# A Mamba and SwiGLU layer on one core: squares of the norms spread over beats, softplus split over two beats, one exponential moved up to the table load

## The chip, the cores and the metric

The kernel runs on one core of one Trainium2 chip. The metric is the device time of one execution in microseconds. An engine is called by its name in the profile: PE (TensorE matmul), PEld (its weight load), DVE (VectorE), ACT (ScalarE), POOL (GpSimd), SP (SyncE).

## What is computed

The input has 8192 tokens (4 sequences of 2048) of 256 channels. One layer of two halves is applied to it.

```python
# half 1: selective state space block (D_INNER = 512, N_STATE = 16, DT_RANK = 16, K_CONV = 4)
x_in, res = split(x @ W_in)
x_conv = silu(causal_dw_conv(x_in, conv_w, conv_b))             # u
dt, Bm, Cm = split(x_conv @ W_x)
delta = softplus(dt @ W_dt + b_dt)
h = exp(delta * A) * h + delta * Bm * x_conv                    # scan over tokens, 16 states a channel
y = sum_n(h * C) + u * D
x1 = layernorm(x + (y * silu(res)) @ W_out)
# half 2: gated feed-forward block (HIDDEN = 768, integer weights / 127)
out = layernorm(x1 + (silu(x1 @ Wg.T) * (x1 @ Wu.T)) @ Wd.T)
```

Softplus is computed as max(v, 0) + ln(1 + exp(-|v|)): Relu, Abs, Exp and Ln on ACT. A norm takes the mean (`minus_mean`), four Squares with an accumulator output (one for each 128 tokens), then rstd = exp(-0.5 ln(var + eps)), then a scale and a shift on POOL.

## The kernel before

The tokens are cut into 16 chunks of 512. A step of the loop handles one chunk, and a step has 64 beats: 16 states times 4 blocks of 128 channels. At each beat ACT computes da = exp(A * delta) for one state and block (`exp`, L1052), POOL computes dbu (L1185), and DVE runs the recurrence over 512 tokens (`scan`, L1360, tile `h`). After four beats PE turns the four blocks of the state around (tiles `ht_upper`, `ht_lower`, L699); ACT weighs the upper half with C (`weigh`, L1061, tile `gt`), DVE sums the lower half (L1372, tile `acc`), PE turns the weighed upper half back onto `y_upper` (L724).

All other matmuls are called fills. They go through two PSUM banks in turn (`fill_banks`) at beats written out by hand in `FILL_AT`, and are read at the beats of `READ_AT`. In step i they serve the projections, the convolution and softplus of chunk i+1 (the front) and the output projection, the norms and the feed-forward block of chunk i-1 (the back). A fill waits until its bank's holder before it has been read.

Every engine runs its instructions in the order in which the program lists them. On ACT a beat lists: the exponential of that beat, then `sums` (the weighing, at every beat with beat % 4 = 1 or 3), the norms, the reads of the back, the reads of the front, and at the beats 35 and 45 (`SILUS`) the silu work. There ACT first computes the exponentials of the next two beats (`AHEAD = 2`) into SBUF (`da_ahead`), loads the table of silu (L1129), runs one silu instruction, and in the beat behind it the second, and loads the table of exp and ln again (L1140). The beat that follows (38 or 48) begins with its own exponential. da has two banks, so exp of beat b waits for the scan of beat b-2; dbu has four buffers.

The second norm of a chunk (`which` = 1) falls into the second step behind it, beats 64 and above of `BEAT` counted from the step before: 65 is beat 1, 86 is beat 22. Of the first norm PE transposes the result in the fill `x1t0` at beat 28.

In the traces below a scan is numbered by its beat: the step that is read runs from 929.25 us (scan of beat 0) to 1041.47 us. Of its scans, that of beat 24 begins at 968.93, of 26 at 971.95, of 30 at 978.19, of 38 at 994.23 and of 48 at 1012.75.

Of the kernel before, what the change touches and what calls it, by code (L numbers as in the profile page):

```python
# [12 lines left out]
ACT = mybir.ActivationFunctionType  # L13
# [3 lines left out]
TT = T // P  # L17
# [38 lines left out]

BEAT = {"times u": [53, 55, 58, 63], "x1 low": [33, 34], "mean": [22, 65], "rstd": [23, 65], "shift": [26, 86],
        "norm": [29, 86], "silu uz": 35, "silu gate": 45, "y upper": [6, 6], "times z": [11, 12, 12, 15]}

FIRST_FILLS = ["xin0", "xin1", "xin2", "xin3", "conv2", "conv0", "conv1", "conv3", "dtb", "dt0", "dt1", "ct", "dt2", "dt3"]  # L60

# [13 lines left out]
AHEAD = 2  # L75
SILUS = sorted(BEAT[name] for name in ("silu uz", "silu gate"))
# [2 lines left out]

assert not [n for n, at in READ_AT.items() if n[:2] == "dt" and n != "dtb" and at - 1 in SILUS]  # L80
assert not [b for b in BEAT["rstd"] if b - 1 in SILUS or b - 65 in SILUS]


def due(names, beat):

    return [name for name in names if READ_AT[name] == beat]
# [10 lines left out]
def in_steps(at, beat, first, last):  # L97

    return not (first if beat < at else last)


def tiles_due(kind, beat):

    return [n for n, at in enumerate(BEAT[kind]) if at == beat]


def mamba_swiglu(nc, x, x_t, w_in, conv_w, conv_b, w_x, w_dt, b_dt, a_log, d_skip, w_out, w_gate_t, w_up_t,
# [9 lines left out]
    KK, DB, HB = DM // P, DI // P, HID // P  # L117
# [21 lines left out]
    with ExitStack() as ctx:  # L139
# [32 lines left out]
        u = sb("u", [P, 2, DB, T])  # L172
        z = sb("z", [P, 2, DB, T])
        delta = sb("delta", [P, 2, DB, T])
# [18 lines left out]
        xr = sb("xr", [P, 2, TT, DM])  # L193
# [96 lines left out]
        def ahead(beat):  # L290

            for start in SILUS:
                if start < beat <= start + AHEAD:
                    return beat - start - 1
            return None
# [588 lines left out]
        def _(act):  # L884
# [3 lines left out]
            def front(c, par, beat):  # L888
                if beat == 0:


                    start = T + (HALO if c % PER_SEQ == 0 else 0)
                    after(act, xin_ready, c * (DB + 1))
                    copy(xin[:, :, 0:HALO], xin[:, :, start:start + HALO]).then_inc(xin_ready, 1)
                read_front(c, par, due(F_FILLS, beat))

            def read_front(c, par, names):
                for name in names:
                    m = int(name[-1]) if name[-1].isdigit() else 0
                    b = front_bank(c, name)  # L900
                    act.wait_ge(fp_ready, front_filled(c, name))
                    if name[:3] == "xin":
                        act.wait_ge(xin_ready, c * (DB + 1) + 1)
                        copy(xin[:, m, HALO:HALO + T], b[:, :]).then_inc(xin_ready, 1)
                    elif name[:3] == "res":
                        if isinstance(c, int) and c == 1 and m == 0:

                            act.wait_ge(w_ready, 6)
                        after(act, lower_done, (c - 2) * DP + m // 2 + 1)
                        copy(z[:, par, m, :], b[:, :]).then_inc(res_raw, 1)  # L910
                    elif name[:4] == "conv":

                        after(act, lower_done, (c - 2) * DP + m // 2 + 1)
                        nc.scalar.activation(u[:, par, m, :], b[:, :], ACT.Identity,
                                             bias=convb_s[:, m:m + 1]).then_inc(conv_raw, 1)
                    elif name == "dtb":
                        after(act, b_written, 16 * c)
                        nc.scalar.activation(xd[:, :], b[0:XD, :], ACT.Identity, bias=ones_row[:, 0:1])\
                            .then_inc(xd_ready, 2)
                    elif name == "ct":  # L920
                        copy(ct[:, par, :, :], b[:, 0:TT * NS].rearrange("p (t n) -> p t n", n=NS))\
                            .then_inc(ct_ready, 1)
                    else:

                        d = delta[:, par, m, :]
                        done = (c * DB + m) * 3

                        if c:
                            nc.scalar.activation(du[:, par, m, :], b[:, :], ACT.Relu).then_inc(relu_ready, 1)
                        nc.scalar.activation(d, b[:, :], ACT.Abs).then_inc(softplus_step, 1)  # L930
                        act.wait_ge(softplus_step, done + 1)
                        nc.scalar.activation(d, d, ACT.Exp, scale=-1.0).then_inc(softplus_step, 1)
                        act.wait_ge(softplus_step, done + 2)
                        nc.scalar.activation(d, d, ACT.Ln, bias=1.0).then_inc(softplus_step, 1)


            def silu_u(c, par):
# [12 lines left out]
            def minus_mean(c, which):  # L950
                act.wait_ge((res1_done, res2_done)[which], (c + which + 1) * TT)
                if which:
                    act.wait_ge(nmr_ready, 2 * c + 1)
                elif isinstance(c, int):
                    after(act, nmr_ready, 2 * c)
                nc.scalar.activation(neg_mean[:, :], row_sum[:, which, :], ACT.Copy, scale=-1.0 / DM)\
                    .then_inc(mean_ready, 1)

            def reciprocal_std(c, par, which):

                if which:
                    act.wait_ge(x1_ready, TT * (c + 1))
                elif isinstance(c, int):
                    after(act, o_ready, TT * c)
                act.wait_ge(mean_ready, 2 * c + which + 1)
                for t in range(TT):
                    nc.scalar.activation(squares[:, t, :], xr[:, par, t, :], ACT.Square, bias=neg_mean[:, t:t + 1],
                                         accum_out=sq[:, t:t + 1]).then_inc(sq_done, 1)
                act.wait_ge(sq_done, TT * (2 * c + which + 1))
                nc.scalar.activation(rstd[:, :], sq[:, :], ACT.Ln, bias=eps_s[:, 0:1], scale=1.0 / DM)\  # L970
                    .then_inc(rstd_step, 1)
                act.wait_ge(rstd_step, 2 * (2 * c + which) + 1)
                nc.scalar.activation(rstd[:, :], rstd[:, :], ACT.Exp, scale=-0.5).then_inc(rstd_step, 1)
# [58 lines left out]
            def norms(c, par, beat):  # L1032
                for which in tiles_due("mean", beat):
                    minus_mean(c, which)
                for which in tiles_due("rstd", beat):
                    reciprocal_std(c, par, which)

            def exp(i, par, beat):
                n, m = beat // DB, beat % DB
# [68 lines left out]
            def step(i, par):  # L1108
                first, last = [isinstance(i, int) and i == c for c in (0, NCH - 1)]
                for beat in range(NH):  # L1110

                    if ahead(beat) is None and not (first and beat < 2):
                        exp(i, par, beat)
                    sums(i, par, beat, first, False)
                    if not (isinstance(i, int) and i < 2):
# [22 lines left out]
                        silu_z(0, 0)  # L1138
                    if beat - 1 in SILUS:
                        nc.scalar.preload_act_table_set(EXP_SET)  # L1140

            steps(step)
            for beat in range(NH):
# [382 lines left out]
```

## Time and profile before

| | |
|---|---|
| median of 3 runs | 1870.64 us (1870.13 to 1873.51) |
| profiled execution, span | 1865.8 us |
| a step of 64 beats in that execution (steps 1 to 14) | 112.2 to 112.8 us |
| busy: PE, DVE, POOL, ACT | 1715.3, 1705.4, 1651.8, 1636.9 us |
| scan L1360 on DVE | x1024, 1269 ns each |
| exp da L1052 on ACT | x1024, 689 ns each |
| weigh gt L1061 on ACT | x512, 681 ns each |
| Square L967 on ACT | x120, 498 ns, and 190 ns for each read of the accumulator |
| table loads L1129, L1140 | x32 each, 1283 ns |

The span is the profiled execution from its first to its last instruction; the median of the runs is 4.8 us above it. An idle time in brackets behind an instruction is that of its engine just before it, with what ended it. Ends of PE's instructions are modelled, so that its rows show overlaps: four 128-column transposes are given 0.60 us but start every 0.44 us.

### The profile page before, as it was taken

The numbers are of one execution on the slowest core, as the hardware profiler recorded it, in microseconds if no ns is written. First come the engines' busy times: TensorE is split into PE (matmuls) and PEld (weight loads), VectorE is DVE, ScalarE is ACT, GpSimd is POOL, SyncE is SP. The second block draws the span as 40 slices with busy tenths as digits, with TensorE's granted clock in tenths as the row PEclk, the third lists the DMA queues.
The fourth block names the chain that finished last, engine by engine and source line by source line (L and its number), as shares of the span: only waits on it lengthen the run. The fifth ranks groups of instructions, "written<-read, shape, count | busy, mean of one in ns | idle before, by whom it ended". The sixth has DMA issues, their size and how long they took to land.

```text
span 1865.8 us, 32487 instructions
## 1 busy us (share of the span) xinstructions
PE 1715.3 (92%) x10128; PEld 1287.3 (69%) x10128; DVE 1705.4 (91%) x1958; ACT 1636.9 (88%) x2769; POOL 1651.8 (89%) x1629
## 2 busy tenths in 40 slices
PE   8879898998989999898998989999898998988788
PEld 3546676776767677676776767677676776767667
DVE  5989999999999999999999999999999999999994
ACT  5798988989899898998989899898998989898774
POOL 3989899998989989899898999989899898989970
PEclk9999999999999999999999999999999999999999
DMA  7213123141231314214141231313214041221100
GB/s 240 109 46 136 47 71 134 35 159 47 103 102 58 125 47 142 63 60 145 35 151 55 99 106 58 125 47 135 70 58 147 36 147 57 87 96 41 62 23 24
DMA packets 82107, 164.56 MB, mean 88 GB/s; under 512 B 10369, under 2 KB 28033, under 8 KB 81938
## 3 DMA queue, kind: packets, MB, share of 16 engines
q1 hardware_dynamic: 80498, 160.90, 25.1%
q8 instruction: 85, 1.39, 0.3%
q10 hardware_dynamic: 1440, 1.58, 0.3%
q14 instruction: 84, 0.69, 0.1%
HBM read 87.47 MB, written 8.91 MB: 52 GB/s over the span
## 4 chain that ended last, share of the span: by engine, by line
PE 65%; ACT 22%; POOL 7%; issue 4%; DVE 2%; DMA 0%; DVEq 0%; SPq 0%; ACTq 0%; POOLq 0%
PE fill L524 10%; PE ht_upper L699 9%; PE ht_lower L699 9%; PE y_upper L724 8%; PE fill L639 8%; POOL dbu L1185 6%; PE fill L608 5%; PE fill L629 5%; ACT da L1052 4%; ACT gt L1061 3%; PE fill L539 3%; ACT L1140 2%; ACT L1129 2%; PE fill L578 2%; ACT kb L948 2%
## 5 line engine op out<-in xcount | busy, mean ns | idle before, releaser
L1185 POOL TENSOR_TENSOR dbu<-du,brep 128x512 f32<-128x512 f32 x1024 | 1310.6, 1306 | 152.3 <-DVE h L1360 128.7
L1360 DVE TENSOR_TENSOR_SCAN h<-da,carry,dbu 128x512 f32<-128x512 f32 x960 | 1186.9, 1269 | 92.5 <-ACT da L1052 90.7
L1052 ACT ACTIVATE da<-delta,a_s 128x512 f32<-128x512 f32 x960 | 655.7, 689 | 97.2 <-DVE h L1360 89.8
L1061 ACT ACTIVATE gt<-ht_upper,ct 128x512 f32<-128x512 f32 x512 | 348.5, 681 | 62.7 <-PE ht_upper L699 55.7
L699 PE MATMUL ht_upper<-ident,h 128*128 128x128 f32 x2048 | 317.7, 278 | 67.7 <-DVE h L1360 57.3
L699 PEld LDWEIGHTS ht_upper<-ident,h 128*128 128x128 f32 x2048 | 245.9, 143 | 185.9 <-DVE h L1360 102.8
L1372 DVE SCALAR_TENSOR_TENSOR acc<-ht_lower,ct,acc 128x512 f32<-128x512 f32 x480 | 348.6, 726 | 22.4 <-PE ht_lower L699 22.4
L699 PE MATMUL ht_lower<-ident,h 128*128 128x128 f32 x2048 | 317.0, 278 | 39.4 <-DVE acc L1372 34.9
L724 PE MATMUL y_upper<-ident,gt 128*128 128x128 f32 x2048 | 316.6, 278 | 0.0
L699 PEld LDWEIGHTS ht_lower<-ident,h 128*128 128x128 f32 x2048 | 243.8, 143 | 103.0 <-issue 50.4
L724 PEld LDWEIGHTS y_upper<-ident,gt 128*128 128x128 f32 x2048 | 245.8, 143 | 72.1 <-ACT gt L1061 39.6
L524 PE MATMUL fill<-xt_s,win_s 128*128 128x512 f32 x456 | 217.5, 594 | 0.1
L639 PE MATMUL fill<-wd_s,kb 128*128 128x256 f32 x720 | 180.4, 380 | 0.7 <-DVE xr L1272 0.5
L639 PEld LDWEIGHTS fill<-wd_s,kb 128*128 128x128 f32 x720 | 125.8, 190 | 19.2 <-DVE xr L1272 8.0
L629 PE MATMUL fill<-x1t,wg_s 128*128 128x512 f32 x360 | 128.8, 471 | 3.3 <-ACT kb L1000 3.2
L608 PE MATMUL fill<-wout_s,kb 128*128 128x256 f32 x480 | 118.5, 380 | 0.0
L629 PE MATMUL fill<-x1t,wu_s 128*128 128x512 f32 x360 | 110.2, 428 | 4.1 <-ACT delta L930 4.1
L524 PEld LDWEIGHTS fill<-xt_s,win_s 128*128 128x128 f32 x456 | 76.8, 190 | 51.5 <-issue 50.8
L1360 DVE TENSOR_TENSOR_SCAN h<-da_ahead,carry,dbu 128x512 f32<-128x512 f32 x64 | 101.0, 1617 | 0.0
L608 PEld LDWEIGHTS fill<-wout_s,kb 128*128 128x128 f32 x480 | 87.6, 190 | 10.4 <-issue 0.4
L307 POOL TENSOR_TENSOR du<-delta,u 128x512 f32<-128x512 f32 x60 | 76.5, 1276 | 4.7
L629 PEld LDWEIGHTS fill<-x1t,wg_s 128*128 128x128 f32 x360 | 69.2, 222 | 16.5 <-ACT kb L1000 9.3
(189 smaller groups left out, 1871.9 us busy)
## 6 DMA issues: line engine op xcount, KB each, us to landing
brep<-b_rows SPq DMA_DIRECT2D x127, 512.0 KB, 3.8
xs<-xin SPq DMA_DIRECT2D x242, 256.0 KB, 2.5
xr<-x SPq DMA_DIRECT2D x16, 512.0 KB, 4.2
xt_s<-x_t SPq DMA_DIRECT2D x15, 512.0 KB, 5.1
out<-xr SPq DMA_DIRECT2D x15, 512.0 KB, 3.9
win_s<-w_in SPq DMA_DIRECT2D x2, 512.0 KB, 5.0
h<-xin SPq DMA_DIRECT2D x4, 256.0 KB, 4.0
h<-xin ACTq DMA_DIRECT2D x4, 256.0 KB, 4.5
```

What stands on the lines that cost most here:

```text
L307: unit.tensor_tensor(du[:, par, m, :], d, u[:, par, m, :], ALU.mult).then_inc(du_ready, 1)
L524: mm = nc.tensor.matmul(front_bank(c, name)[:, :], win_s[:, k, m * P:(m + 1) * P], xt_place(c)[:, k, :], start=(k == 0), stop=(k == KK - 1))
L608: mm = nc.tensor.matmul(fill_bank(name)[:, 0:DM], kb[:, m, t * P:(t + 1) * P], wout_s[:, m, :], start=(m == 0), stop=(m == DB - 1))
L629: mm = nc.tensor.matmul(fill_bank(name)[:, :], w[:, k, n * P:(n + 1) * P], x1t[:, half, k, :], start=(k == 0 and half == 0), stop=(k == KK ...
L639: mm = nc.tensor.matmul(fill_bank(name)[:, 0:DM], kb[:, n, t * P:(t + 1) * P], wd_s[:, n, :], start=(n == 0), stop=(n == HB - 1))
L699: mm = nc.tensor.transpose(bank[:, m * P:(m + 1) * P], h[:, n % 2, m, t * P:(t + 1) * P], ident[:, :])
L724: mm = nc.tensor.matmul(y_upper[m // 2][:, (m % 2) * HALF + k * P:(m % 2) * HALF + (k + 1) * P], lhsT=gt[:, (n * UPPER + k) % GT, m * P:(m ...
L1052: nc.scalar.activation(dst[:, :], delta[:, par, m, :], ACT.Exp, scale=a_s[:, m, n:n + 1])\
L1061: nc.scalar.activation(gt[:, (n * UPPER + k) % GT, :], ht_upper[:, :], ACT.Copy, scale=ct[:, par, k, n:n + 1])\
L1185: nc.gpsimd.tensor_tensor(dbu[:, beat % DBU, :], du[:, par, m, :], brep[:, n // PIECE % 2, n % PIECE, :], ALU.mult).then_inc(dbu_ready, 1)
L1360: nc.vector.tensor_tensor_scan(h[:, n % 2, m, 0:T], da[beat % 2][:, :] if slot is None else da_ahead[:, slot, :], dbu[:, beat % DBU, :], c ...
L1372: nc.vector.scalar_tensor_tensor(out=acc[:, par, k, :], in0=ht_lower[:, :], scalar=ct[:, par, UPPER + k, n:n + 1], in1=acc[:, par, k, :], ...
```

## The change

Three things are done, all in the order of ACT's instructions, with POOL's `shift` following the first.

1. The four Squares of a norm no longer stand in one beat with the Ln and Exp of rstd. First norm: mean 22, squares 22, 23, 24, 25, rstd 25 (was 23), shift 27 (was 26), norm 29 as before. Second norm: mean 76 (was 65), squares 77, 79, 81, 82, rstd 83 (was 65), shift 84 (was 86), norm 86 as before.
2. Exp and Ln of softplus of a `dt` block move from the beat that reads it (49, 51, 55, 59) to the next beat, behind that beat's exponential da. For chunk 0 they stay.
3. The exponential of beats 38 and 48, the first that is not computed ahead of a silu, moves from the start of its beat to the end of beat 36 or 46, directly behind the table load.

The number and sizes of all instructions stay the same.

```diff
-BEAT = {"times u": [53, 55, 58, 63], "x1 low": [33, 34], "mean": [22, 65], "rstd": [23, 65], "shift": [26, 86],
-        "norm": [29, 86], "silu uz": 35, "silu gate": 45, "y upper": [6, 6], "times z": [11, 12, 12, 15]}
+BEAT = {"times u": [53, 55, 58, 63], "x1 low": [33, 34], "mean": [22, 76], "square": [(22, 23, 24, 25), (77, 79, 81, 82)],
+        "rstd": [25, 83], "shift": [27, 84], "norm": [29, 86], "silu uz": 35, "silu gate": 45, "y upper": [6, 6],
+        "times z": [11, 12, 12, 15]}
...
+AFTER_SILU = [start + AHEAD + 1 for start in SILUS]
...
+def squares_due(which, beat):
+
+    return [t for t, at in enumerate(BEAT["square"][which]) if at == beat]
...
                 read_front(c, par, due(F_FILLS, beat))
+                for m in range(DB):
+                    if READ_AT[f"dt{m}"] + 1 == beat:
+                        softplus(c, par, m)
...
                         if c:
                             nc.scalar.activation(du[:, par, m, :], b[:, :], ACT.Relu).then_inc(relu_ready, 1)
-                        nc.scalar.activation(d, b[:, :], ACT.Abs).then_inc(softplus_step, 1)
-                        act.wait_ge(softplus_step, done + 1)
-                        nc.scalar.activation(d, d, ACT.Exp, scale=-1.0).then_inc(softplus_step, 1)
-                        act.wait_ge(softplus_step, done + 2)
-                        nc.scalar.activation(d, d, ACT.Ln, bias=1.0).then_inc(softplus_step, 1)
+                        nc.scalar.activation(delta[:, par, m, :], b[:, :], ACT.Abs).then_inc(softplus_step, 1)
+                        if not c:
+                            softplus(c, par, m)
+
+            def softplus(c, par, m):
+
+                d = delta[:, par, m, :]
+                done = (c * DB + m) * 3
+                act.wait_ge(softplus_step, done + 1)
+                nc.scalar.activation(d, d, ACT.Exp, scale=-1.0).then_inc(softplus_step, 1)
+                act.wait_ge(softplus_step, done + 2)
+                nc.scalar.activation(d, d, ACT.Ln, bias=1.0).then_inc(softplus_step, 1)
...
+            def square(c, par, which, t):
+
+                act.wait_ge(mean_ready, 2 * c + which + 1)
+                nc.scalar.activation(squares[:, t, :], xr[:, par, t, :], ACT.Square, bias=neg_mean[:, t:t + 1],
+                                     accum_out=sq[:, t:t + 1]).then_inc(sq_done, 1)
+
+            def reciprocal_std(c, which):
 
                 if which:
                     act.wait_ge(x1_ready, TT * (c + 1))
                 elif isinstance(c, int):
                     after(act, o_ready, TT * c)
-                act.wait_ge(mean_ready, 2 * c + which + 1)
-                for t in range(TT):
-                    nc.scalar.activation(squares[:, t, :], xr[:, par, t, :], ACT.Square, bias=neg_mean[:, t:t + 1],
-                                         accum_out=sq[:, t:t + 1]).then_inc(sq_done, 1)
...
                 for which in tiles_due("mean", beat):
                     minus_mean(c, which)
+                for which in range(2):
+                    for t in squares_due(which, beat):
+                        square(c, par, which, t)
                 for which in tiles_due("rstd", beat):
-                    reciprocal_std(c, par, which)
+                    reciprocal_std(c, which)
...
-                    if ahead(beat) is None and not (first and beat < 2):
+                    if ahead(beat) is None and beat not in AFTER_SILU and not (first and beat < 2):
                         exp(i, par, beat)
...
                     if beat - 1 in SILUS:
                         nc.scalar.preload_act_table_set(EXP_SET)
+                        exp(i, par, beat + AHEAD)
```

## Rows read from the trace of the kernel before

**Rows 1.** Page, parts 1 and 4: busy time of each engine; shares of the chain.
```profile
PE 1715.3 (92%) x10128; PEld 1287.3 (69%) x10128; DVE 1705.4 (91%) x1958; ACT 1636.9 (88%) x2769; POOL 1651.8 (89%) x1629
...
PE 65%; ACT 22%; POOL 7%; issue 4%; DVE 2%; DMA 0%; DVEq 0%; SPq 0%; ACTq 0%; POOLq 0%
```

**Rows 2.** Busy in three stretches of one step: span, PE, PEld, DVE, ACT, POOL, clock, DMA.
```profile
929.20:980.60 51.40, 50.61 (x311) 36.22 (x308) 48.40 (x55) 44.78 (x89) 50.81 (x55) 1.00 0.42 143
980.60:1015.10 34.50, 28.59 (x163) 21.61 (x163) 31.05 (x32) 34.21 (x48) 26.96 (x25) 0.95 0.15 50
1015.10:1041.40 26.30, 26.22 (x158) 21.84 (x159) 25.61 (x34) 23.09 (x39) 25.99 (x25) 1.00 0.13 42
```

**Rows 3.** Timeline of PE, beats 31 to 36: start, duration, work, idle time before it.
```profile
980.60 0.66 PE L617 MATMUL fill<-ident,xr 128*128 128x128 f32 x4 [0.73 <-ACT z L886]
...
984.57 0.63 PE L699 MATMUL ht_lower<-ident,h 128*128 128x128 f32 x4 [1.38 <-DVE acc L1372]
...
988.04 1.11 PE L699 MATMUL ht_upper<-ident,h 128*128 128x128 f32 x4 [2.40 <-DVE h L1360]
```

**Rows 4.** Timeline of ACT, beats 22 to 32.
```profile
967.15 0.50 ACT L967 ACTIVATE kb<-xr,stats 128x256 bf16<-128x256 f32 x1
...
968.22 0.68 ACT L1052 ACTIVATE da<-delta,a_s 128x512 f32<-128x512 f32 x1
...
970.08 0.69 ACT L1061 ACTIVATE gt<-ht_upper,ct 128x512 f32<-128x512 f32 x1
970.67 0.59 ACT L886 ACTIVATE z<-fill 128x512 f32<-128x512 f32 x1
971.15 0.70 ACT L1052 ACTIVATE da<-delta,a_s 128x512 f32<-128x512 f32 x1
...
975.13 0.60 ACT L886 ACTIVATE z<-fill 128x512 f32<-128x512 f32 x1 [0.70 <-PE fill L524]
...
980.44 1.30 ACT L1052 ACTIVATE da<-delta,a_s 128x512 f32<-128x512 f32 x2
```

**Rows 5.** Timeline of DVE, scans of beats 26 to 32.
```profile
971.95 2.62 DVE L1360 TENSOR_TENSOR_SCAN h<-da,carry,dbu 128x512 f32<-128x512 f32 x2
...
978.19 2.59 DVE L1360 TENSOR_TENSOR_SCAN h<-da,carry,dbu 128x512 f32<-128x512 f32 x2
...
981.33 2.45 DVE L1360 TENSOR_TENSOR_SCAN h<-da,carry,dbu 128x512 f32<-128x512 f32 x2
```

**Rows 6.** Timeline of all engines behind the first silu, beats 37 to 39.
```profile
992.93 0.69 ACT L1061 ACTIVATE gt<-ht_upper,ct 128x512 f32<-128x512 f32 x1
993.51 0.68 ACT L1052 ACTIVATE da<-delta,a_s 128x512 f32<-128x512 f32 x1
...
993.76 0.63 PE L699 MATMUL ht_upper<-ident,h 128*128 128x128 f32 x4 [0.77 <-ACT gt L1061]
...
994.23 2.46 DVE L1360 TENSOR_TENSOR_SCAN h<-da,carry,dbu 128x512 f32<-128x512 f32 x2 [1.98 <-ACT da L1052]
...
994.61 0.69 ACT L1052 ACTIVATE da<-delta,a_s 128x512 f32<-128x512 f32 x1
...
996.44 1.21 PE L629 MATMUL fill<-x1t,wg_s 128*128 128x512 f32 x4 [0.25 <-ACT kb L1000]
```

**Rows 7.** Timeline of all engines behind the second silu, beats 47 to 50.
```profile
1011.44 0.69 ACT L1061 ACTIVATE gt<-ht_upper,ct 128x512 f32<-128x512 f32 x1
...
1012.03 0.69 ACT L1052 ACTIVATE da<-delta,a_s 128x512 f32<-128x512 f32 x1
...
1012.36 0.60 PE L699 MATMUL ht_upper<-ident,h 128*128 128x128 f32 x4
...
1015.07 1.20 PE L629 MATMUL fill<-x1t,wu_s 128*128 128x512 f32 x4 [0.30 <-ACT delta L930]
...
1015.71 0.63 ACT L934 ACTIVATE delta<-delta 128x512 f32<-128x512 f32 x1
...
1016.60 1.26 POOL L305 TENSOR_TENSOR delta<-delta,du 128x512 f32<-128x512 f32 x1
```

More of the change, by code:

```diff
@@ L81 @@
 assert not [b for b in BEAT["rstd"] if b - 1 in SILUS or b - 65 in SILUS]
+assert all(len(at) == TT and at[-1] <= BEAT["rstd"][n] for n, at in enumerate(BEAT["square"]))
+AFTER_SILU = [start + AHEAD + 1 for start in SILUS]
 def due(names, beat):
@@ L923, in read_front @@
                     else:
-                        d = delta[:, par, m, :]
-                        done = (c * DB + m) * 3
                         if c:
                             nc.scalar.activation(du[:, par, m, :], b[:, :], ACT.Relu).then_inc(relu_ready, 1)
-                        nc.scalar.activation(d, b[:, :], ACT.Abs).then_inc(softplus_step, 1)
-                        act.wait_ge(softplus_step, done + 1)
-                        nc.scalar.activation(d, d, ACT.Exp, scale=-1.0).then_inc(softplus_step, 1)
-                        act.wait_ge(softplus_step, done + 2)
-                        nc.scalar.activation(d, d, ACT.Ln, bias=1.0).then_inc(softplus_step, 1)
+                        nc.scalar.activation(delta[:, par, m, :], b[:, :], ACT.Abs).then_inc(softplus_step, 1)
[8 more added lines that the diff above has]
+                nc.scalar.activation(d, d, ACT.Ln, bias=1.0).then_inc(softplus_step, 1)
             def silu_u(c, par):
@@ L957, in minus_mean @@
                     .then_inc(mean_ready, 1)
-            def reciprocal_std(c, par, which):
+            def square(c, par, which, t):
[3 more added lines that the diff above has]
+            def reciprocal_std(c, which):
                 if which:
```

## The prediction

> **What bounds the kernel now.** I read the page first: PE, DVE, POOL and ACT are busy 92, 91, 89 and 88% of the span, so shares of busy time decide nothing, but the chain that ended last runs over PE for 65% of the span, over ACT for 22, over POOL for 7 and over DVE for 2 [rows 1]. Next come the windows of one step of the steady part, 929.2 to 1041.4 us [rows 2]. The reader is to see that one step has three stretches with different bounds. From 929.2 to 980.6 (beats 0 to 31) PE is busy 50.61 of 51.40 us, and 0.73 us of the rest is a single wait at its end [rows 3]: PE runs through its own list without a pause, while ACT is idle for 6.6 us. From 1015.1 to 1041.4 it is busy 26.22 of 26.30. Between them, from 980.6 to 1015.1, PE is idle for 5.9 us and ACT is busy 34.21 of 34.50: here ACT with its two pairs of silus sets the time. So a step costs what PE has to do, 105.4 us, and what PE waits in the middle stretch. A stall of DVE costs something only where PE has to wait for it, and a saving of ACT gains something only if a wait of PE in the middle gets shorter. That is how I price each part.
>
> **Squares of the second norm** (beat 1 to beats 13, 15, 17, 18). Four Squares with the Ln and Exp leave ACT where it is late for its exponentials, and come in where it is idle. DVE's scans of beats 2 to 8 wait less. But both places lie in the first stretch, where PE does not wait [rows 2]. Value: 0. Bounds: from -0.1 us a step (the sum of PE's pauses there, 51.40 - 50.61 - 0.73) to +0.3, since POOL's `shift` now stands at beat 20, one beat behind the Ln and Exp at 19, and `dbu` of the next beats is queued behind it on an engine that is itself busy 50.81 of 51.40 us.
>
> **Squares of the first norm** (all at beat 23 to 22, 23, 24, 25, rstd from 23 to 25). ACT's list at beat 25 is da25, the weighing, and now one Square, Ln and Exp, and then the read `z` and da26. The weighing at 970.08 depends on PE's transposes and cannot move, as PE sets the time there. Before, `z` followed at 970.67 and da26 at 971.15 [rows 4]. The last Square, Ln and Exp take 968.22 - 967.15 = 1.07 us until the exponential behind them can start [rows 4]. So da26 starts at 972.22 and ends at 972.92, and the scan of beat 26, which began at 971.95 [rows 5], begins 1.0 us later. The same work had been ahead of the weighing before; it is put behind a wait. ACT itself is back on its old times by 975.13, where it had waited 0.70 us [rows 4]; DVE is not, as it has no pause between 971.95 and 980. I take 0.8 us for its delay at beat 30 (978.99 instead of 978.19) and 0.14 less at the end of scan 31, since the pair of scans at 978.19 took 2.59 us where one without a wait takes 2.45 [rows 5]: 980.78 + 0.66 = 981.44. The exponential of beat 33, which needs the bank of scan 31, is the second of the pair at 980.44; it ends at 981.74, lasts 0.69 and so began at 981.05 [rows 4]. It now begins at 981.47, 0.4 us later, and it stands in the stretch where ACT sets the time. PE's waits for DVE's `acc` at 984.57 (1.38 us) and for its scan at 988.04 (2.40 us) grow with it [rows 3]. Value: +0.4 us a step. Bounds: 0 (DVE makes the delay up) and +0.8 (none is made up). The `shift` at 27 and the norm at 29 on POOL keep some tenths to the transposes of `x1t0`; I put them at 0.
>
> **The exponential next to the table load.** This is the part that looks like a gain. DVE waited 1.98 us for da38 [rows 6]. With da38 ahead of the weighing, the scan of beat 38 begins 993.51 - 992.93 = 0.58 us sooner. But ACT has the same work to do before da39, which still starts at 994.61 and ends at 995.30; scan 39 began at 994.23 + 2.46 - 1.27 = 995.42, 0.12 behind that [rows 6]. DVE gains 0.1 and no more. What moves is the weighing: it ends 0.6 us later, and PE waited for just this one, 0.77 us, before `ht_upper` at 993.76, with two more groups of transposes and two fills queued behind [rows 6]. PE was stopped once more, by 0.25 us, at 996.44 [rows 6], which is the cover: +0.6 - 0.25 = +0.35 us. Behind 996.44 PE and ACT hand the work to each other without a pause, so that this delay reaches the second silu. There the same move delays the weighing that ended at 1011.44 + 0.69 = 1012.13. PE answered such an end after 993.76 - 993.62 = 0.14 us [rows 6], and began `ht_upper` at 1012.36 [rows 7]: a cover of 0.09, so PE is 0.5 later. The fill at 1015.07 had waited 0.30 us for the read of `dt0` [rows 7], so that 0.2 us are left; from there PE sets the time for the rest of the step. Value of both moves: +0.55 us a step, bounds +0.1 and +0.8.
>
> **Softplus in two beats.** The two short waits between Abs, Exp and Ln are worth 0.03 us each. The order puts da50 ahead of Exp and Ln, about 0.6 us, and DVE would get da50 sooner; but it stands in the last stretch, where PE sets the time. Ln at 1015.71 ends at 1016.34 and POOL's `times u` began at 1016.60 [rows 7]: it now has to wait until about 1016.95, and the `dbu` of the next beats are queued behind it, on an engine busy 25.99 of 26.30 us [rows 2]. Value: 0, as DVE is no closer than that to POOL in most beats. Bounds: -0.1 (the waits) and +0.35.
>
> **The sum.** 0.4 + 0.35 + 0.2 = 0.95 us a step, in the 14 steps (1 to 14) that have a front and a back: 13.3 us. The first step has no back and the last no front; I give them nothing, with 1 us either way. The profiled execution was 1865.8 us, so I expect 1879.1 for its span; it lies 4.8 below the median of 1870.64, which becomes 1883.9.
>
> **The rivals.**
> (a) DVE is the bound, and the change does what it is for: scans 38 and 48 begin 0.58 us earlier each and nothing gives it back. 14 x 1.16 = 16 us less, 1854. For it: DVE is busy 91%, and waits 1.98 us at a place that is shortened [rows 1, 6]. It decides if scan 39 can follow scan 38 at once; against it stands that da39 ended only 0.12 us before scan 39, and that PE has no pause in two of the three stretches. A rule of the Trainium skill speaks for this rival: its page Perfetto Trace Analysis, section Identifying the Most-Contended Engine, says to take the engine with the highest occupancy, and not to take TensorE's matmul busy share for it but that of its weight loads. Here that share is 69% against DVE's 91% [rows 1], so that by this rule DVE is the engine to relieve and the change would be faster. I go by the starts of PE's instructions, which leave no room in those stretches. Smaller gains, 3 to 8 us, belong here too: PE's waits in the middle shrink a little because ACT is nowhere late before them.
> (b) The delays are absorbed: PE's `ht_upper` groups have more room than their starts show, or DVE makes up its delay before beat 33. Then it is 1870.6, within 3 us.
> (c) POOL becomes the bound: its later `times u` and `shift` add 0.35 us or more a step. 5 us above the forecast, 1889.
> (d) PE's clock. In the middle stretch the granted clock was 0.95 in the mean, which is the lower level of 1.2 GHz for a while [rows 2], and the four transposes behind the idle 2.40 us took 1.11 us where those at 980.60 took 0.66 [rows 3]. The forecast adds idle time of PE at 993 and at 1012. If that brings a second such stretch, its price is that of the first, 0.05 x 34.5 = 1.7 us a step, and behind 1012 nothing hides it: 24 us more, 1908. The Trainium skill has the rule for it (TensorE: Matmul & The Clock Gate, Part 1: The HAM clock gate): an idle TensorE is set to 1.2 GHz and activity releases it. The trace agrees for the wait of 2.40 us; the waits of 0.77 and less left no lower clock behind, which is why the chance is small.
>
> **How the numbers follow.** The forecast has 0.62, with its own range 1875 to 1889 (0.3 to 1.3 us a step); (c) has 0.06, (d) 0.05, (b) 0.10, (a) 0.17, of which about 0.06 are the small gains. The likeliest time is 1883.9. The range is 1866 to 1891: it leaves out (d) and the large gain of (a). A measurement of this kernel can tell about 0.2%, 3.7 us, from no change. Faster by more than that: 0.17. Within it: 0.10. Slower: 0.73.
>
> **What would show it.** Right: the idle time of PE before `ht_upper` behind the first silu grows from 0.77 to over 1 us and a new one of about 0.8 us stands behind the second; DVE's wait for da38 falls from 1.98 us to about 1.4 and a new wait of about 0.9 us appears at beat 26; ACT stays without pauses in the middle stretch, and a step takes about 113.2 us. Wrong: a step below 112 us, or no new wait of PE; then the bound was not read rightly. DVE's waits at beats 2 to 8, 56 and 60 should shrink in any case, and the step is not to follow them.

## The result, and the profile after

The changed kernel takes 1879.29 us (1877.98 to 1880.06), against 1870.64 us for the kernel before. The medians differ by 8.65 us; the ratio of the runs is 1.0041, 95% interval 1.0029 to 1.0054. The forecast was 1883.9, with 1866 to 1891 as its range: the sign and the range hold, and of the 13.3 us that were forecast 8.65 came. The profiled execution of after is 1876.2 us long, 10.4 more than the one of before (1865.8). The head of its page:

```profile
span 1876.2 us, 32487 instructions
PE 1727.5 (92%) x10128; PEld 1300.5 (69%) x10128; DVE 1711.2 (91%) x1958; ACT 1623.6 (87%) x2769; POOL 1653.4 (88%) x1629
```

The busy shares moved by a point at most from [rows 1], so they say nothing about the cause. The windows of one step do, with the columns of [rows 2]. This step starts (scan of beat 0) at 936.12 us where that of before started at 929.25; 6.87 us are to be taken off a time of after to lay it over one of before.

```profile
936.10:987.50 51.40, 50.72 (x308) 36.10 (x306) 47.78 (x53) 44.13 (x89) 50.26 (x55) 1.00 0.38 138
987.50:1022.40 34.90, 29.24 (x162) 22.26 (x162) 32.25 (x33) 34.32 (x48) 28.62 (x26) 0.90 0.19 56
1022.40:1048.80 26.40, 26.40 (x160) 22.21 (x160) 25.37 (x34) 22.77 (x39) 25.05 (x24) 1.00 0.13 41
```

The first stretch is as long as before, 51.40 us, and PE is busy 50.72 of it. The middle one is 34.90 us instead of 34.50. The last begins 0.4 us later and is as full of PE as it was. So the time is lost in the middle, as forecast, but less of it. PE's idle time there did not grow, though: it is 5.66 us instead of 5.91, while PE is busy 0.65 us more at a granted clock of 0.90 instead of 0.95. That is what rival (d) looks like, but it is not the cause. In the steps 13 and 14 of after the lower level lasts 3.4 us, in the steps 1 to 11 it lasts 6.8, and a typical step takes 112.70 us with either.

The places that the prediction named, DVE first (timeline of DVE; the last bracket is the idle time before the instruction and what ended it). They are the scans of beat 26, of 38, of 39, and of 48 behind the second silu.

```profile
979.57 2.47 DVE L1381 TENSOR_TENSOR_SCAN h<-da,carry,dbu 128x512 f32<-128x512 f32 x2 [1.31 <-ACT da L1072]
...
1000.73 1.28 DVE L1381 TENSOR_TENSOR_SCAN h<-da,carry,dbu 128x512 f32<-128x512 f32 x1 [1.20 <-ACT da L1072]
...
1002.41 1.28 DVE L1381 TENSOR_TENSOR_SCAN h<-da,carry,dbu 128x512 f32<-128x512 f32 x1 [0.39 <-ACT da L1072]
...
1019.33 2.59 DVE L1381 TENSOR_TENSOR_SCAN h<-da,carry,dbu 128x512 f32<-128x512 f32 x2 [1.04 <-ACT da L1072]
```

Beat 26 has the new wait, 1.31 us. Beat 38 waits 1.20 instead of 1.98 us [rows 6], but the next scan then waits 0.39 us for da39, as that exponential is no earlier than it was: the gain of da38 is handed back one beat later. The cause of the new wait stands in ACT's timeline of beat 25:

```profile
976.67 0.69 ACT L1081 ACTIVATE gt<-ht_upper,ct 128x512 f32<-128x512 f32 x1 [1.20 <-PE ht_upper L707]
977.25 0.50 ACT L977 ACTIVATE kb<-xr,stats 128x256 bf16<-128x256 f32 x1
...
977.93 0.30 ACT L987 ACTIVATE stats<-stats,eps_s 128x4 f32<-128x4 f32 x1
978.26 0.21 ACT L990 ACTIVATE stats<-stats 128x4 f32<-128x4 f32 x1
978.38 0.58 ACT L894 ACTIVATE z<-fill 128x512 f32<-128x512 f32 x1
978.86 0.68 ACT L1072 ACTIVATE da<-delta,a_s 128x512 f32<-128x512 f32 x1
```

ACT stands idle for 1.20 us until PE has turned the state, then weighs it, and only then comes the last Square with Ln and Exp. Between the weighing and `z` there are now 978.38 - 976.67 = 1.71 us, where there were 0.59 [rows 4]: the 1.1 us of the norm lie behind a wait instead of ahead of it, while ACT idled for as long.

Now PE (timeline of PE): its waits at beats 31, 33 and 35, then `ht_upper` behind the first and behind the second silu.

```profile
987.50 0.66 PE L625 MATMUL fill<-ident,xr 128*128 128x128 f32 x4 [0.60 <-ACT z L894]
...
991.86 0.63 PE L707 MATMUL ht_lower<-ident,h 128*128 128x128 f32 x4 [1.51 <-DVE acc L1393]
...
995.33 1.11 PE L707 MATMUL ht_upper<-ident,h 128*128 128x128 f32 x4 [2.41 <-DVE h L1381]
...
1001.45 0.63 PE L707 MATMUL ht_upper<-ident,h 128*128 128x128 f32 x4 [0.41 <-ACT gt L1081]
...
1020.05 0.63 PE L707 MATMUL ht_upper<-ident,h 128*128 128x128 f32 x4 [0.52 <-ACT gt L1081]
```

The first three brackets hardly differ from [rows 3], and the one behind the first silu is smaller, 0.41 instead of 0.77 us [rows 6]. It is the starts that tell the delay. Less 6.87 us they are 980.63, 984.99, 988.46, 994.58 and 1013.18; before they were 980.60, 984.57, 988.04, 993.76 and 1012.36 [rows 3, 6, 7]. So PE is 0.03 us late at beat 31, 0.42 at 33 and 35, 0.82 at the first group behind each silu. Not all of that stays: at beat 40 it is 0.28, and from beat 52 to 62 it is 0.35 to 0.46 us.

Where the 10.4 us of the profiled executions lie, read as the time from each step's beat-0 scan to the next one's (here and in the experiments; some steps are longer than their neighbours, mostly by a wait that is treated below, so "typical" is the median of those steps of 2 to 13 that are within 0.1 us of the shortest of them):

| profiled execution | ahead of the first scan | first step | typical step | steps 1 to 14 | last step and tail | span |
|---|---|---|---|---|---|---|
| before | 33.6 | 109.92 | 112.21 | 1572.1 | 150.2 | 1865.8 |
| after | 34.1 | 112.81 | 112.70 | 1578.3 | 151.0 | 1876.2 |

A typical step takes 0.49 us more (forecast: 0.95), the fourteen together 6.2, the first step 2.9 (forecast: nothing, with 1 us either way), the rest 1.3. Most of the first step's share lies at one place, before the fills of beat 40. Before:

```profile
97.10 0.63 PE L699 MATMUL ht_upper<-ident,h 128*128 128x128 f32 x4
...
97.10:101.90 4.80, 4.80 (x21) 2.84 (x22) 4.33 (x5) 4.39 (x8) 3.18 (x4) 1.00 0.00 0
```

and after, the timeline's row and the window:

```profile
98.24 0.63 PE L707 MATMUL ht_upper<-ident,h 128*128 128x128 f32 x4 [2.03 <-ACT gt L1081]
...
98.20:104.70 6.50, 6.46 (x20) 3.70 (x21) 4.03 (x5) 3.82 (x7) 3.93 (x4) 0.74 0.00 0
```

There the weighing, put behind its exponential, let PE stand for 2.03 us, and the granted clock of the 6.5 us that follow is 0.74 in the mean, that is, the lower level of 1.2 GHz for half of them. In this stretch PE is busy without a pause in both kernels (4.80 of 4.80 us and 6.46 of 6.50), so the slower matmuls cost their whole length: counted from the start of the step, PE is 0.61 us late where it begins and 2.30 where it ends. Not every such wait leaves the lower level behind: in the first step of before one of 2.41 us, at 122.07 us, is followed by a granted clock of 1.00.

### The profile page after: what moved, and what is told of

It reads as the page before. It is cut to its first block, busy times and chain, and to the rows that moved or that the text cites. A ratio compares the mean times of both kernels' runs of the same rounds, so it can differ in the third digit from the quotient of the medians.

```text
span 1876.2 us, 32487 instructions
## 1 busy us (share of the span) xinstructions
PE 1727.5 (92%) x10128; PEld 1300.5 (69%) x10128; DVE 1711.2 (91%) x1958; ACT 1623.6 (87%) x2769; POOL 1653.4 (88%) x1629
## 4 chain that ended last, share of the span: by engine, by line
PE 69%; ACT 15%; POOL 9%; issue 5%; DVE 1%; DMA 0%; DVEq 0%; SPq 0%; POOLq 0%; ACTq 0%
PE ht_upper L707 10%; PE fill L532 10%; PE ht_lower L707 9%; PE y_upper L732 9%; PE fill L647 8%; POOL dbu L1206 7%; PE fill L637 6%; PE fill L616 5%; ACT gt L1081 3%; PE fill L547 3%; ACT L1160 2%; ACT L1149 2%; PE fill L586 2%; ACT da L1072 2%; PE fill L568 1%
## 5 line engine op out<-in xcount | busy, mean ns | idle before, releaser
L313 POOL TENSOR_TENSOR delta<-delta,du 128x512 f32<-128x512 f32 x60 | 76.7, 1278 | 16.0 <-ACT delta L949 16.0
```

## The experiments

Two readings stood against each other. By the first, that of the prediction, PE's list sets the steady step, and each part costs what it delays PE in the middle stretch. By the second, DVE sets it, and each part costs or gains what the scans lose or win. Beside them the first step and the clock were open. No kernel here leaves out any part of the computation.

**The three parts, one at a time.** Squares alone, softplus alone, the exponential alone:

```diff
 # e1_squares: only the positions of the squares, rstd and shift
-"mean": [22, 65], "rstd": [23, 65], "shift": [26, 86]
+"mean": [22, 76], "square": [(22, 23, 24, 25), (77, 79, 81, 82)], "rstd": [25, 83], "shift": [27, 84]
 # e2_softplus: only Exp and Ln one beat behind Relu and Abs
+for m in range(DB):
+    if READ_AT[f"dt{m}"] + 1 == beat:
+        softplus(c, par, m)
 # e3_exp_next: only the exponential at the load
-if ahead(beat) is None and not (first and beat < 2):
+if ahead(beat) is None and beat not in AFTER_SILU and not (first and beat < 2):
...
+exp(i, par, beat + AHEAD)
```

> Part 1 alone: the Squares of both norms spread, softplus and the exponential as before. Theory P (PE sets the time, a delay counts where PE waits from start to start): the Squares put behind ACT's wait at beat 25 delay PE by 0.5 to 0.7 us in the middle of a step, and as softplus is as before nothing gives it back at the turn of the step: 14 x 0.5 to 0.7 = +7 to +10 us, 1878 to 1881. Theory T (what the changed kernel gives back at the turn of a step, 0.45 us, comes from the Squares that left beat 1): +0 to +4 us, 1871 to 1875.

> Part 2 alone: Exp and Ln of softplus one beat behind Relu and Abs. Theory P with the wait for da60 as what holds DVE and then PE at the turn of a step: PE's group of transposes there starts 0.73 us behind the one before it instead of 0.44, and 0.07 more at the group before; that goes, -0.3 to -0.4 us a step, -4 to -6 us, 1865 to 1867. Theory T: no gain at the turn, and POOL's longer wait for Ln costs 0 to 0.3 us a step: 1870 to 1875.

> Part 3 alone: the exponentials of beats 38 and 48 directly behind the table load. Theory P: PE waits for the weighing behind it; in the steps with a front and a back +0.1 (first silu) and +0.2 (second), 14 x 0.3 = +4 us, and in the first step a longer wait of PE (0.15 to about 2 us) with a second stretch at the lower clock behind it, +2.3: in all +6 us, 1876 to 1878. The theory that DVE is the bound: two scans 0.58 us earlier in each step, 16 us less, 1854.

Measured, as a ratio to the kernel before on the same chip: squares 1.0018 (1.0010 to 1.0027), softplus 0.9988 (0.9979 to 0.9996), the exponential 1.0041 (1.0029 to 1.0053). Typical steps: 112.67, 112.07 and 112.45 us, so +0.46, -0.15 and +0.24 us; their sum, +0.55, is the +0.49 of the whole change, within 0.06. In e3_exp_next PE's first `ht_upper` behind the first silu is 0.63 us late, but the groups from beat 40 on only 0.10; behind the second silu it is 0.63 and then 0.24. So 0.10 and 0.14 us stay, not 0.35 and 0.2. It also carries the first step's loss, 112.39 us against 109.92, and has the longest tail of these executions (154.5 us), which the median need not share.

(In e2_softplus half of the steps 2 to 13 are such longer ones, and the median of all twelve is 112.22 us, that of before; the gain is read from the undisturbed half and from the ratio.)

The gain of softplus is a surprise, and it shows where time had been hidden. The turn of the step on PE, before:

```profile
1039.79 0.60 PE L639 MATMUL fill<-wd_s,kb 128*128 128x256 f32 x2
1040.29 0.66 PE L699 MATMUL ht_upper<-ident,h 128*128 128x128 f32 x4
1041.02 0.63 PE L699 MATMUL ht_lower<-ident,h 128*128 128x128 f32 x4
```

and the same groups in e2_softplus:

```profile
480.63 0.60 PE L647 MATMUL fill<-wd_s,kb 128*128 128x256 f32 x2
481.06 0.60 PE L707 MATMUL ht_upper<-ident,h 128*128 128x128 f32 x4
481.50 0.60 PE L707 MATMUL ht_lower<-ident,h 128*128 128x128 f32 x4
481.94 1.88 PE L532 MATMUL fill<-xt_s,win_s 128*128 128x512 f32 x4
```

Neither shows a wait in brackets. But from start to start the three groups take 0.43, 0.44 and 0.44 us in e2_softplus, and before they took 0.50 and 0.73: 0.36 us of waiting that PE's rows do not show as idle, because the modelled end of a matmul reaches over it. The rows of the weight loads do show idle time there, 0.30 us before the load of `ht_upper`, released by DVE's `h`, and 0.29 before that of `ht_lower`. With softplus in two beats DVE begins its scans of beats 60 to 63 0.5 us sooner, counted back from the next step's start, and this wait is gone. Only part of it stays a gain: counted from the next step's start PE is 0.40 us early 3 us into it, and 0.16 from 6 us on.

**The first norm by itself, and without its wait.** The squares of the second norm stay where they were. In one kernel the first norm ends at beat 25, behind the weighing, as in the change; in the other at beat 24, which has no weighing:

```diff
 # e5_first_norm
+"square": [(22, 23, 24, 25), (65, 65, 65, 65)], "rstd": [25, 65], "shift": [27, 86]
 # e6_first_norm_ahead
+"square": [(22, 23, 24, 24), (65, 65, 65, 65)], "rstd": [24, 65], "shift": [27, 86]
```

> The spread of the first norm alone (Squares at 22, 23, 24, 25, rstd 25); second norm, softplus and exponentials as before. A full step took 112.22 us before in most steps, 112.67 with the Squares of both norms spread. Theory Q (the last Square, Ln and Exp behind ACT's wait at beat 25 make the scans from beat 26 late by 1 us, and PE by 0.6 at beats 31 to 36): the whole loss is the first norm's, 112.6 to 112.9 us a step, 1876 to 1880 us. Rival R (POOL, which waits for the second norm's rstd at beat 20, is what costs): 112.2 us a step, 1871 to 1873.

> The first norm spread, but with its last Square, Ln and Exp at beat 24, ahead of the weighing that waits for PE (Squares 22, 23, 24, 24, rstd 24, shift 27); all else as before. Theory Q: the scans from 26 on are on their old times within 0.2 us and a step takes 112.2 to 112.3, 1871 to 1873 us. Rival S (it is the Squares at 22 and 23 that make da23 and the reads late, wherever the last stands): 112.6 or more a step, 1876 or more.

Measured: 1.0046 (1.0034 to 1.0058) and 1.0006 (0.9996 to 1.0016), typical steps 112.71 and 112.21 us against 112.21. The whole loss of the squares is the first norm's, +0.49 us a step, and the second norm's take 0.04 off it again. The totals differ by more: e5_first_norm lies 0.28%, 5 us, above e1_squares, where the steps explain under 1 us. Their profiled executions have tails of 153.7 and 149.0 us; what makes them so is not shown. In general the totals of this section agree with what the steps add up to within about 4 us only, and the argument goes by the steps. The scan of beat 26 in e5_first_norm has the wait of after:

```profile
979.85 2.47 DVE L1376 TENSOR_TENSOR_SCAN h<-da,carry,dbu 128x512 f32<-128x512 f32 x2 [1.31 <-ACT da L1068]
```

In e6_first_norm_ahead it has none. There DVE even began its scan at beat 24 earlier than before, at 968.56 instead of 968.93 us, 0.35 earlier in a step that starts at 929.23 instead of 929.25, because an exponential was no longer behind four Squares:

```profile
968.56 1.28 DVE L1376 TENSOR_TENSOR_SCAN h<-da,carry,dbu 128x512 f32<-128x512 f32 x1
970.02 1.28 DVE L1376 TENSOR_TENSOR_SCAN h<-da,carry,dbu 128x512 f32<-128x512 f32 x1 [0.18 <-ACT da L1068]
...
980.57 0.66 PE L625 MATMUL fill<-ident,xr 128*128 128x128 f32 x4 [0.73 <-ACT z L894]
984.54 0.63 PE L707 MATMUL ht_lower<-ident,h 128*128 128x128 f32 x4 [1.38 <-DVE acc L1388]
...
988.01 1.07 PE L707 MATMUL ht_upper<-ident,h 128*128 128x128 f32 x4 [2.40 <-DVE h L1376]
```

PE's waits at beats 31 to 35 are those of [rows 3], each begun 0.03 us sooner, which is the start of the step. That shows that the order of ACT behind its wait is the whole cause, not the spreading of the squares. The 0.35 us that DVE had won bought nothing, but this does not tell the two readings apart: the next scan waits 0.18 us for its exponential, which begins when it did before (969.30 against 969.31), and by beat 27 all is handed back. It is the same as with da38 and da39.

**Which engine sets the step.** One more group of transposes for PE in a step (0.44 us), and one more instruction for DVE:

```diff
 # e8_pe_more, in the turning of the upper half
+if n == 3 and k == 0:
+    turn(ht_upper, n, k)
 # e9_dve_more, in the scan
+if beat == 13:
+    nc.vector.tensor_copy(spare_tile[:, :], ident[:, 0:1].broadcast_to([P, T]))
```

> The kernel before with one more group of four transposes on PE in each step (the upper half of the fourth state is turned twice, at beat 16), 0.44 us of work where PE has no pause. If PE sets the time there: +0.44 us in each of the 14 full steps, +6 us, 1877 to 1879. If DVE sets the time: nothing, 1871 to 1873.

> The kernel before with one more copy of 512 columns on DVE in each step, ahead of the scan of beat 13 (0.2 to 0.6 us; it writes a tile of its own). If PE sets the time at beats 0 to 31: PE's groups of transposes from beat 16 on keep their times and a step stays at 112.2, 1870 to 1874 us. If DVE sets it: the copy's own duration in each step, +3 to +8 us.

Measured: 1.0051 (1.0039 to 1.0063) for PE's group, typical step 112.65 us, +0.44, which is all of it. DVE is shifted by the same 0.44 us from beat 24 on; its sum `acc` there, which waited 0.77 us for PE, waits 1.21:

```profile
974.98 0.75 DVE L1390 SCALAR_TENSOR_TENSOR acc<-ht_lower,ct,acc 128x512 f32<-128x512 f32 x1 [1.21 <-PE ht_lower L707]
```

DVE's copy took more than its expectation had assumed (0.2 to 0.6 us):

```profile
959.16 1.14 DVE L1378 COPY spare_tile<-ident 128x512 f32<-128x512 f32 x1
```

The next scan is 1.07 us later. PE is 0.47 us late at its group at 965.29 us (beat 16), 0.78 from beat 20 on, and does not make it up; the typical step is 113.01, +0.80 us, and the ratio 1.0084 (1.0070 to 1.0097). Both forecasts of this run were too low. So the first reading is right only up to 0.28 us: by so much DVE may fall behind at beats 13 to 20 before PE waits for it. A stall of DVE of 1 us costs even in the stretch where PE is busy without a pause. The two engines are tied, and neither reading holds alone.

**The first step.** The old order at the load in the first step only:

```diff
-if ahead(beat) is None and beat not in AFTER_SILU and not (first and beat < 2):
+if ahead(beat) is None and (beat not in AFTER_SILU or first) and not (first and beat < 2):
...
-exp(i, par, beat + AHEAD)
+if not first:
+    exp(i, par, beat + AHEAD)
```

> All of the change, but in the first step the exponentials of beats 38 and 48 stay where they were. Theory C (with the moved exponential PE waits 2 us at beat 38 of the first step, is given the lower clock behind it, and a fill there takes 2 us longer): the first step takes 109.9 to 110.6 us instead of 112.8, and the whole 2 to 2.5 us less than the changed kernel, 1876 to 1878. Rival: the first step is as long as in the changed kernel, since POOL waits there for the later Ln of softplus: 112 to 113 us, no difference.

Measured: 1.0045 (1.0033 to 1.0057), no better than the change in the median. In its profile the jump at beats 39 to 42 is gone (the delay against before is 1.03 us at both). Of the fourteen profiles exactly the three that move the exponential there in the first step (after, e3_exp_next, e12_first_silu) have it, 2.40 us each, so the exponential's place does cause it. But the same execution has another loss in the first step, 1.35 us of waiting before a convolution fill at beat 21, and its step is 111.37 us long. The intervals of both ratios are over 2 us to either side, so that the medians can neither show nor exclude the 2.4 us. Only one of the two moves, the one at the first silu, was taken alone too:

```diff
-AFTER_SILU = [start + AHEAD + 1 for start in SILUS]
+AFTER_SILU = [start + AHEAD + 1 for start in SILUS[:1]]
```

> Only the exponential of beat 38 moved up to the table load, that of beat 48 as before. The trace of part 3 alone had PE 0.10 us late behind the first silu and 0.14 more behind the second: a step of 112.3 instead of 112.46, 14 x 0.1 = +1.4 us, and the first step +2.3 through PE's wait and clock at its beat 38: 1873 to 1877 us. If the loss sits at the second silu alone: a step of 112.2 and a first step of 110, 1871 to 1873.

Measured: 1.0022 (1.0010 to 1.0034), typical step 112.31, +0.09 us, first step 112.47. The first step's 2.5 us and 14 times 0.09 are 3.8 us, and the ratio gives 4.1. So the move at the first silu costs 0.1 us a step and, once, 2.5 us in the first step; the move at the second adds the rest of e3_exp_next.

**The waits that come and go.** Single steps are 0.6 to 0.8 us longer than their neighbours in most of the kernels, though in none of the steps 2 to 14 of after. In the trace it is mostly one fill of the convolution, here in e2_softplus:

```profile
403.63 1.06 PE L547 MATMUL fill<-xs,taps 128*32 128x512 f32 x8 [0.60 <-issue]
```

It is held up when the last of the four DMAs that write the shifted `xin` lands 33.9 to 34.1 us into the step instead of 32.1 to 32.9; the fill stands at 33.4 to 33.5. A kernel with this fill one beat later:

```diff
-"conv2": (20,)
+"conv2": (21,)
```

> The kernel before with the convolution fill conv2 at beat 21 instead of 20, behind one group of transposes. Theory D (the 0.6 to 0.7 us by which single steps are longer in some executions, and 1.4 us in the first step, are PE's wait for the DMA that shifts xin for this fill): no step is longer than the others by 0.6 at beat 22, the scatter of the runs shrinks and the median falls by 1 to 3 us, 1868 to 1871. Rival: the long steps come from the clock or from elsewhere and stay: no change, 1871 to 1874.

Measured: 0.9996 (0.9986 to 1.0007). Most of the long steps are gone from the trace, but the times scatter as before, 1867.3 to 1874.3 us. This wait is real and is not what makes the executions differ. The last step with the tail, 149.0 to 154.5 us in these profiles, may be the larger part of it, but they are one profile for each kernel and cannot show it. Nor is the length of a first step alone a proof: that of e4_softplus_second below is 112.85 us without any moved exponential, through a wait of 1.40 us before a convolution fill.

**Only what helped.** Softplus in two beats, and the squares of the second norm spread while the first norm stays where it was; then the same with the later convolution fill:

```diff
 # e4_softplus_second
+"mean": [22, 76], "square": [(23, 23, 23, 23), (77, 79, 81, 82)], "rstd": [23, 83], "shift": [26, 84]
 # e11_best: e4_softplus_second and
+"conv2": (21,)
```

> Part 2 and the Squares of the second norm alone (beats 13, 15, 17, 18); first norm and exponentials as before. Theory P: the second norm is worth nothing where PE has no wait, so the time is that of part 2 alone, 1865 to 1867, within 1 us of it. Theory T: here the gain at the turn appears, 0.45 us a step, and it is 6 us faster than part 2 alone.

> What helped or did no harm, together: softplus in two beats, the Squares of the second norm at beats 13, 15, 17, 18, conv2 at beat 21; first norm and exponentials as before. Softplus and the second norm brought a step from 112.22 to 112.05, theory D takes 1 to 3 us more: 1866 to 1869 us, faster than before by 0.15 to 0.3%. If the parts undo each other: 1869 to 1872.

Measured: 0.9982 (0.9972 to 0.9991), typical step 111.99, and 0.9973 (0.9964 to 0.9982), 1866.70 us beside 1872.29 for the kernel before on that chip, typical step 111.92. The second has the lowest time of the study and is faster than both kernels of the case; its interval overlaps that of the first. Its page:

```profile
span 1865.4 us, 32487 instructions
PE 1720.5 (92%) x10128; PEld 1300.8 (70%) x10128; DVE 1704.3 (91%) x1958; ACT 1620.9 (87%) x2769; POOL 1651.8 (89%) x1629
```

Its shares are again those of all the others.

## Why the prediction was right or wrong

**Squares of the second norm: 0 was right.** They gain a little, within the bound of -0.1: 0.08 us a step between e2_softplus and e4_softplus_second, which differ by them alone, and 0.04 between e5_first_norm and e1_squares. In e4_softplus_second PE keeps the lead that softplus gives it (0.47 us early at 8 to 13 us into the step, instead of 0.16) and loses part of it later (0.26 from 16 us on).

**Squares of the first norm: the mechanism was right, the size a little low.** In e5_first_norm, which has them alone, the scan of beat 26 begins 1.05 us later than before (1.0 was worked out; the wait of 1.31 is longer, as DVE comes to it 0.35 us earlier, as in e6_first_norm_ahead), that of beat 30 is 0.84 us late (0.8 was taken), and the exponential of beat 33 begins 0.46 us later (0.42 was worked out):

```profile
987.62 1.44 ACT L1068 ACTIVATE da<-delta,a_s 128x512 f32<-128x512 f32 x2
```

It is the second of the pair and lasts 0.69, so it begins at 988.37, 52.26 us into its step; before it began at 51.80. PE is 0.70 us late at beats 33 and 35, but there it waits 1.50 and 2.41 us, and from beat 40 on 0.49 are left. That is the step's +0.49 instead of 0.4. POOL, put at 0, waits 1.15 us at `shift` for the Exp of beat 25; whether that adds to the step is not shown.

**The exponential: the mechanism was right, the terms were too large.** It costs 0.10 us behind the first silu instead of 0.35, and 0.14 behind the second instead of 0.2. The step of the prediction that failed is the cover. The delay of 0.6 us at `ht_upper` came (0.63 in e3_exp_next), but the prediction took the idle 0.25 us at 996.44 [rows 6] for all the room that PE had behind it. From one `ht_upper` to the next PE took, before and in e3_exp_next:

```profile
993.76 0.63 PE L699 MATMUL ht_upper<-ident,h 128*128 128x128 f32 x4 [0.77 <-ACT gt L1061]
...
995.02 1.17 PE L629 MATMUL fill<-x1t,wg_s 128*128 128x512 f32 x4
996.44 1.21 PE L629 MATMUL fill<-x1t,wg_s 128*128 128x512 f32 x4 [0.25 <-ACT kb L1000]
997.49 0.60 PE L699 MATMUL ht_upper<-ident,h 128*128 128x128 f32 x4
```

```profile
1113.23 0.63 PE L707 MATMUL ht_upper<-ident,h 128*128 128x128 f32 x4 [0.58 <-ACT gt L1077]
...
1114.49 2.10 PE L637 MATMUL fill<-x1t,wg_s 128*128 128x512 f32 x8
1116.43 0.60 PE L707 MATMUL ht_upper<-ident,h 128*128 128x128 f32 x4
```

That is 3.73 us before and 3.20 with the later start: the room was 0.53 us, twice what the bracket says. The same room takes 0.2 us off the delay of the first norm (0.70 to 0.49 in e5_first_norm). That da38 earlier brings DVE nothing, because da39 is no earlier, was right; the row at 1002.41 shows it.

**Softplus: 0 was wrong, and its bound too.** It gains 0.15 us a step (the bound was -0.1). The prediction said that the last stretch gives PE no room, since PE is busy 26.22 of its 26.30 us [rows 2]; 0.36 us of waiting were inside that busy time. In after the same place gives back as much: PE is 0.46 us late at beat 62 and 0.10 at the last group before the next step. So of the missing 0.46 us a step (0.95 less 0.49) the exponential's terms account for 0.31, softplus for 0.15 and the second norm for 0.04, against 0.09 more on the first norm; 0.05 us stay unassigned.

**The first step: nothing, with 1 us either way, was wrong.** It takes 2.9 us, 2.4 of them the exponential's. This is rival (d) at a single place, where the prediction had looked for it only in the steady step. The rule of the Trainium skill that was cited there (TensorE: Matmul & The Clock Gate, Part 1: The HAM clock gate) agrees with the wait of 2.03 us that left the lower clock behind; by the length of the wait alone it can't be told, as one of 2.41 us left none. In the steady step the lower clock lasted longer too, mean 0.90 against 0.95 in the middle stretch, and cost nothing, as ACT sets the time there: in the kernel before too, steps with 6.8 us at the lower level are as long as those with 3.4, 112.2 us.

**The sum: in part luck.** The forecast gave all of its 13.3 us to the fourteen steps. They took 6.2; the first step, the start and the tail, put at nothing, brought another 4.2 in the profiled executions. Of the 4.6 us between the forecast and the measured median 2.9 are the span, and 1.7 come from the distance between span and median: it is 3.1 us for after, where the 4.8 of before was taken over.

**The rivals.** (a) fell as a forecast: the scans behind the silus hand their gain back, and the time went up. But its condition was nearer than the prediction says, with 0.28 us between PE and DVE at beats 13 to 20. The rule of the Trainium skill named beside it (Perfetto Trace Analysis, Identifying the Most-Contended Engine) would have chosen DVE alone; here 0.44 us more on PE cost 0.44 us a step, so that relieving DVE alone could not be enough. (b) fell, but a part of it came true: 0.2 of the 0.70 us of the first norm and 0.5 of the 0.63 of the exponential were absorbed behind the first silu. (c): POOL waits for the later Ln (1.04 us at `times u` in after); in the steady steps no loss of its own could be seen. The first step of e2_softplus is 0.44 us longer than before; whether POOL is why is not shown.

**What should have shown it.** The new wait at beat 26, the shorter one at 38 and the step shorter than 113.2 but above 112 came. The wait of PE behind the first silu over 1 us did not: 0.41 in the step shown and 0.85 to 0.88 in steps where the lower clock is short, with PE 0.8 us late at that group in both. The new wait behind the second silu is 0.52 us, not 0.8. A wait at one place is the delay less what has piled up earlier, and was a poor marker; the start would have been a good one.

## What to carry to other kernels

Read PE from start to start against an undisturbed group of the same shape; the idle time in the record left out 0.3 to 0.4 us of waiting here, as ends are modelled, and a stretch that looks full may have room. An instruction moved on an in-order engine is to be placed by what waits ahead of it: ahead of a wait the norm's 1.1 us were free, and behind it they cost 0.5 us a step. The first and the last round of a pipelined loop need a pricing of their own, since work that hides a wait or a slow clock in the steady round is missing there.

## What the runs showed of the hardware that was not expected

- A table load of 1.28 us was followed by its exponential at once. In the second silu of after (timeline of ACT):

```profile
1017.31 1.28 ACT L1160 ACT_TABLE_LOAD   x1
1018.61 0.69 ACT L1072 ACTIVATE da<-delta,a_s 128x512 f32<-128x512 f32 x1
```

- DVE's copy of one broadcast column into 128 x 512 f32 took 1.14 us, nearly as long as a scan over the same shape (1.27).
- The same DMA lands up to 1.9 us later in some steps of the same execution, with the same program; why stays open.
- How long PE stays at the lower clock level behind the same wait differs between steps of one execution, 3.4 or 6.8 us. In the last step with the tail the lower level takes 7.5 to 25.7 us in all, by profile. What decides that is open too.
